# Local attention in a fused six-layer kernel: the loop over layers written out, and the weight split of a layer spread over two steps

## What is computed

```python
for i in range(DEPTH):
    x = attn_layer(shift_tokens(x), Wqkv[i], q_scale[i], k_scale[i], Wo[i]) + x
    x = ffn_layer(shift_tokens(x), ln_g[i], ln_b[i], W1[i], b1[i], W2[i], b2[i]) + x
...
def attn_layer(x, Wqkv, qs, ksc, Wo):
    qkv = x @ Wqkv                       # Wqkv is 128 x 3072
    ...                                  # l2norm of q and k, rotation, local attention
    return out @ Wo
```

## Time and profile before

| | us |
|---|---|
| median of 3 runs | 4807.92 (4804.89 to 4809.58) |
| the profiled execution | 4799.15, its span 4797.3 |
| PE, DVE, ACT, POOL busy in the span | 4226.0, 4007.1, 3749.9, 3518.3 |
| phase B, first to last step mark | 573.7 to 4045.5 |
| a plain step, n odd and n even | 35.33 and 36.02 |
| the two steps after a convert step | 36.02 and 35.33 |

### The profile page before, as it was taken

The page is one execution under the profiler, slowest core; times in us unless marked ns, Lnnn a source line. Parts: engine busy times, 40 slices in busy tenths (PEclk is TensorE's granted clock), DMA queues, the critical chain, the costliest instruction groups (busy, mean ns, idle before and its releaser), DMA issues. The chain is left out here.

```text
span 4797.3 us, 131407 instructions
## 1 busy us (share of the span) xinstructions
PE 4226.0 (88%) x45166; PEld 3150.4 (66%) x45166; DVE 4007.1 (84%) x7658; ACT 3749.9 (78%) x11543; POOL 3518.3 (73%) x2504
## 2 busy tenths in 40 slices
PE   6988699998999989998889989999899998688887
PEld 3555477776777777776777767777677776354553
DVE  4776798888888888888888888898898895688887
ACT  2555588888888888888888888888888887677774
POOL 0100699988899888998989989899899995344444
PEclk9999799999999999999999999999999999788888
DMA  1000111111111111111111111111121111000000
GB/s 27 6 5 2 49 48 44 44 38 52 53 40 43 48 48 47 44 44 45 46 53 43 40 45 52 47 44 44 45 53 38 44 44 28 3 4 3 3 3 5
DMA packets 118641, 169.38 MB, mean 35 GB/s; under 512 B 26563, under 2 KB 44422, under 8 KB 118022
## 3 DMA queue, kind: packets, MB, share of 16 engines
q1 hardware_dynamic: 109246, 160.92, 12.7%
q10 hardware_dynamic: 8776, 0.45, 0.1%
HBM read 20.79 MB, written 2.10 MB: 5 GB/s over the span
## 5 line engine op out<-in xcount | busy, mean ns | idle before, releaser
L1377 POOL TENSOR_TENSOR b_w<-b_w,b_vt 128x512 f32<-128x512 f32 x768 | 1188.4, 1558 | 331.8 <-DVE b_vt L1289 184.1
L1381 POOL TENSOR_TENSOR b_rn<-b_ssm,all_neg_half 128x16 f32<-128x16 f32 x384 | 1171.7, 3051 | 32.0
L1174 ACT ACTIVATE b_Pr<-ps,b_nm 128x96 f32<-128x96 f32 x3072 | 1002.8, 353 | 3.4 <-DVE b_nm L1346 2.8
L1174 ACT ACTIVATION_READ_ACCUMULATOR b_Pr<-ps,b_nm 128x1 f32 x3072 | 677.1, 220 | 0.0
L1216 ACT ACTIVATE b_PT<-ps 96x512 f32<-96x512 f32 x768 | 458.1, 597 | 264.1 <-PE ps L1026 257.1
L1060 PE MATMUL ps<-b_Whi,b_xlo 128*128 128x512 f32 x1152 | 579.2, 503 | 61.7 <-DVE b_Wlo L1306 25.8
L989 PE MATMUL ps<-all_ident,b_w 128*128 128x128 f32 x3072 | 460.6, 281 | 182.3 <-DVE b_xtok L282 118.7
L1340 DVE TENSOR_TENSOR b_Pr<-b_Pr,b_rinv 128x384 f32<-128x384 f32 x768 | 547.0, 712 | 26.3
L1026 PE MATMUL ps<-all_ident,b_Pr 128*96 128x128 f32 x3072 | 479.2, 279 | 68.8 <-ACT b_PT L1216 47.1
L1287 DVE TENSOR_TENSOR b_w<-ps,until_b_rotab 128x512 f32<-128x512 f32 x768 | 524.0, 682 | 8.9 <-ACT b_sq L1193 5.4
L1346 DVE TENSOR_REDUCE b_nm<-ps 128x8 f32<-128x768 f32 x384 | 367.5, 957 | 190.8 <-PE ps L1015 184.6
(11 more groups left out here) (259 smaller groups left out, 9375.4 us busy)
## 6 DMA issues: line engine op xcount, KB each, us to landing
b_V<-b_Vraw SPq DMA_DIRECT2D x384, 192.0 KB, 2.6
b_V<-b_Vraw SPq DMA_DIRECT2D x384, 128.0 KB, 2.4
b_V<-b_Vraw SPq DMA_DIRECT2D x192, 64.0 KB
b_Wraw<-in_L_ffn_Wqkv SPq DMA_DIRECT2D x36, 256.0 KB, 3.4
b_Wo<-in_L_ffn_Wo SPq DMA_DIRECT2D x6, 512.0 KB, 4.5
a_xtok<-in_L_attn_hidden_states SPq DMA_DIRECT2D x16, 128.0 KB, 2.1
out<-c_xout SPq DMA_DIRECT2D x16, 128.0 KB, 1.8
b_W<-in_L_ffn_W SPq DMA_DIRECT2D x6, 341.0 KB, 3.3
```

The lines of the kernel that those rows point to most:

```text
L1174: last = nc.scalar.activation(s.Pr[:, r % 2, j, i], ps[:, S_BANK[j], i * KEYS:(i + 1) * KEYS], ACT.Exp, bias=s.nm[:, r, j, i:i + 1], accum ...
L1377: nc.gpsimd.tensor_tensor(rows, rows, s.vt[:, i % 4], ALU.add).then_inc(s.pool_add, 1)
L1381: nc.gpsimd.tensor_tensor(s.rn[:, j], s.ssm[:, j], g.neg_half[:, 0:HB], ALU.pow).then_inc(s.pool_r, 1)
```

## The change

Two things are done, both in phase B.

The function that lays out the steps has no hardware loop any more: all 100 steps are written out, and every wait, address and table index is a constant. `prefetch` is called in the same four-steps-in places.

The conversion of the chunks is spread over two steps. k = 0 and 1 of the next layer are converted in the step of a layer's last item (n = 16 l + 14), in slots 11 and 14, after the pieces that still use those columns (ACT waits for them by `proj_done`). In the convert step k = 2, 3, 4, 5 stand in slots 1, 4, 7, 10. The last two places of `CHUNKS` change over. The first layer has no step before it and converts k = 0 and 1 in its slot 0. SP's code, its order of transfers and the loads' own conditions are as they were.

```diff
--- before.py
+++ after.py
@@ -716,8 +716,10 @@
 QK_SLOT = {0: (0, 0), 2: (0, 2), 6: (1, 0), 8: (1, 2), 16: (0, 1), 17: (0, 3), 22: (1, 1), 24: (1, 3)}
 V_SLOT = {15: (0, 4), 21: (1, 4), 29: (0, 5), 30: (1, 5)}
 ROTATE_LAG, ADD_LAG = 2, 2
-CHUNKS = (0, 2, 4, 1, 5, 3)
-CONVERT_SLOT = {0: (0, 1), 4: (2,), 8: (3,), 10: (4,), 12: (5,)}
+CHUNKS = (0, 2, 4, 1, 3, 5)
+FIRST_SLOT = {0: (0, 1)}
+AHEAD_SLOT = {11: (0,), 14: (1,)}
+CONVERT_SLOT = {1: (2,), 4: (3,), 7: (4,), 10: (5,)}
 
 LATE_SLOT = {0: (0, 3), 4: (0, 1), 6: (1, 3), 7: (1, 1)}
 WO_SLOT = (11, 12)
@@ -772,8 +774,9 @@
 
 
 
-    def __init__(self, n, odd, front, tail, ffn, closing, half=None, convert=False, edge=None):
+    def __init__(self, n, odd, front, tail, ffn, closing, half=None, convert=False, edge=None, last=False):
         self.n, self.odd, self.front, self.tail, self.ffn, self.closing, self.convert, self.edge = n, odd, front, tail, ffn, closing, convert, edge
+        self.last = last
         every = len(spare_uses(True, True, True, True, True))
         if half is None:
             self.attn, self.vacant = stages_of(n)[1], n == 2
@@ -785,6 +788,17 @@
             start = sum(len(spare_uses(*stages_of(i))) for i in range(-1, 2))
             self.halves, self.first = every * half, start + (every if odd else 0) - 2 * every
 
+    def converted(self, slot):
+
+        pieces = []
+        if self.last:
+            pieces += [(self.front[0] + 1, k) for k in AHEAD_SLOT.get(slot, ())]
+        if self.convert:
+            if self.n == -1:
+                pieces += [(self.front[0], k) for k in FIRST_SLOT.get(slot, ())]
+            pieces += [(self.front[0], k) for k in CONVERT_SLOT.get(slot, ())]
+        return pieces
+
     def spare(self, use):
 
         i = self.first + self.uses.index(use)
@@ -807,31 +821,15 @@
 
 
 def phase_b_steps(engine, body, between=None):
-    def whole(n):
+    for n in range(-1, ITEMS + 3):
         stages = stages_of(n)
         items = [divmod(n + d, NB) if there and n + d >= 0 else None for d, there in zip((1, 0, -1, -2, -3), stages)]
-        body(Step(n, n % 2, items[0], items[2], items[3], items[4], convert=n == -1))
-
-    def inner(l):
-        for pair in range(1, NB // 2 - 1):
-            n, half = NB * l + 2 * pair + 1, NB // 2 * l + pair
-            body(Step(n, 1, (l, 2 * pair + 2), (l, 2 * pair), (l, 2 * pair - 1), (l, 2 * pair - 2), half))
-            body(Step(n + 1, 0, (l, 2 * pair + 3), (l, 2 * pair + 1), (l, 2 * pair), (l, 2 * pair - 1), half + 1))
-
-    for n in range(-1, 3):
-        whole(n)
-    with engine.Fori(0, DEPTH - 1) as l:
-        if between is not None:
-            between(l)
-        inner(l)
-        n, half = NB * l + NB - 1, NB // 2 * l + NB // 2 - 1
-        body(Step(n, 1, (l + 1, 0), (l, NB - 2), (l, NB - 3), (l, NB - 4), half, convert=True, edge=0))
-        body(Step(n + 1, 0, (l + 1, 1), (l, NB - 1), (l, NB - 2), (l, NB - 3), half + 1, edge=1))
-        body(Step(n + 2, 1, (l + 1, 2), (l + 1, 0), (l, NB - 1), (l, NB - 2), half + 1, edge=2))
-        body(Step(n + 3, 0, (l + 1, 3), (l + 1, 1), (l + 1, 0), (l, NB - 1), half + 2, edge=3))
-    inner(DEPTH - 1)
-    for n in range(ITEMS - 1, ITEMS + 3):
-        whole(n)
+        layer, at = divmod(n, NB)
+        if between is not None and at == 3 and 0 <= layer < DEPTH - 1:
+            between(layer)
+        edge = at + 1 if 1 <= layer < DEPTH and at < 3 else None
+        body(Step(n, n % 2, items[0], items[2], items[3], items[4], convert=items[0] is not None and items[0][1] == 0, edge=edge,
+                  last=items[0] is not None and items[0][1] == NB - 1 and items[0][0] + 1 < DEPTH))
 
 
 def phase_b(nc, g, d, ps):
@@ -1176,13 +1174,14 @@
                     last.then_inc(s.exp_done, 1)
 
                 for slot in range(STEP_SLOTS):
-                    if step.convert:
-                        for k in CONVERT_SLOT.get(slot, ()):
-                            c = CHUNKS[k]
-                            act.wait_ge(s.wqkv_in[k % RAW], 16 * (WCHUNKS // RAW) * step.front[0] + 16 * (k // RAW) + 16)
-                            if k == 0:
-                                wait(act, s.proj_done, N_PIECES * f)
-                            nc.scalar.activation(s.Whi[:, c * 512:(c + 1) * 512], s.Wraw[:, k % RAW], ACT.Copy).then_inc(s.whi_done, 1)
+                    for layer, k in step.converted(slot):
+                        c = CHUNKS[k]
+                        act.wait_ge(s.wqkv_in[k % RAW], 16 * (WCHUNKS // RAW) * layer + 16 * (k // RAW) + 16)
+                        if step.last:
+                            act.wait_ge(s.proj_done, N_PIECES * f + max(PIECE.index(at) for at in PIECE if (QK_SLOT.get(at) or V_SLOT[at])[1] == c) + 1)
+                        else:
+                            wait(act, s.proj_done, N_PIECES * f)
+                        nc.scalar.activation(s.Whi[:, c * 512:(c + 1) * 512], s.Wraw[:, k % RAW], ACT.Copy).then_inc(s.whi_done, 1)
                     if step.front is not None and slot in PIECE:
                         tt, c = QK_SLOT[slot] if slot in QK_SLOT else V_SLOT[slot]
                         k = PIECE.index(slot)
@@ -1299,11 +1298,10 @@
                                             ALU.mult).then_inc(s.normed_dve, 1)
 
                 for slot in range(STEP_SLOTS):
-                    if step.convert:
-                        for k in CONVERT_SLOT.get(slot, ()):
-                            cols = slice(CHUNKS[k] * 512, (CHUNKS[k] + 1) * 512)
-                            dve.wait_ge(s.whi_done, WCHUNKS * lf + k + 1)
-                            nc.vector.tensor_tensor(s.Wlo[:, cols], s.Wraw[:, k % RAW], s.Whi[:, cols].bitcast(F32), ALU.subtract).then_inc(s.w_ready, 1)
+                    for layer, k in step.converted(slot):
+                        cols = slice(CHUNKS[k] * 512, (CHUNKS[k] + 1) * 512)
+                        dve.wait_ge(s.whi_done, WCHUNKS * layer + k + 1)
+                        nc.vector.tensor_tensor(s.Wlo[:, cols], s.Wraw[:, k % RAW], s.Whi[:, cols].bitcast(F32), ALU.subtract).then_inc(s.w_ready, 1)
                     if step.tail is not None and slot == RES_SLOT:
                         bank = SPARE[step.spare(("wo", 0))[0]]
                         full_spare(("wo", 0))
```

## The result

| | before | after |
|---|---|---|
| median | 4806.26 us (4796.60 to 4812.96, 20 runs) | 4814.1 us (4807.79 to 4820.12, 20 runs) |
| ratio, 95% interval | | 1.0016 (1.0010 to 1.0023) |
| profiled span | 4797.3 us | 4806.0 us |

A forecast was written before the change was run, and what follows sets the result against it. No engine alone bounds the kernel; PE, DVE and POOL hand each other a full load. -15.7 + 5 x (1.5 + 2.3) + 0.5 = +3.8 us on the 4807.92 us median gives 4812 us, range 4794 to 4828.

The forecast's parts named there:

- the boundaries: Last item's step plus convert step between layers, five times: 5 x (1.5 + 2.3) us longer.
- the straight-line steps: 80 looped steps written out with constants: 0.103 us more per step, +8.2 us.
- The turns: Four turns of the loop over layers vanish in straight-line code: -23.9 us.
- the rival of instruction supply: Twice the code, instruction supply stalls engines now and then: +10 to +20 us in all; chance 0.04.
- The last item's step: Two products moved ahead of DVE's residual add: +1.5 us a layer, bounds 1.0 and 1.9.
- The convert step: First step of a layer: PE's 2.31 us wait goes, a load wait comes; 2.3 us longer, bounds 0.6 and 3.5.
- The stall and its price: Convert step, slot 4: ACT waits 9 to 10 us for chunk 3's load, converting at +14.35; residual add at +30.2.
- the prediction's signs: Expected trace signs: convert step 50 us, ACT's third b_Whi idle 8 to 11 us, load 3.5 us behind first copy.
- The clock rival: PE at half clock after its convert-step idle time becomes the bound: 5 x 3 = 15 us more, 4827 us; chance 0.21.
- The free boundary: DVE catches up later or moved products fall into waits: boundary costs zero, sum -15.2, 4793 us; chance 0.13.
- The page's rule alone: Turns go and straight-line steps are as fast as looped ones: -23.9, 4784 us; chance 0.05.

The follow-up runs named there:

- Experiment 1: Against the changed kernel: all steps still written out, but the six conversions in their old slots and the old chunk order; 4780.62 us, 0.9959 of before.
- Experiment 4: Against the changed kernel: k = 2, 3, 4, 5 back in slots 4, 8, 10, 12; k = 0 and 1 stay ahead; 4777.75 us, 0.9949 of before.
- Experiment 6: Against the changed kernel: the last item's step has DVE's two products in slot 24 and both ACT conversions in slot 11; ratio 0.9990 to before.
- experiments 2: Against the changed kernel: loads of k = 3 and 4 issued early, in the last item's step between its two groups of copies; ratio 0.9947 to before.
- Experiment 3: Against the changed kernel: 84 unread transposes added on PE behind the values of slot 6 in five convert steps; 4821.08 us, 1.0042 of before.

## Why the prediction was right, and which of its terms were off

The forecast of a small loss made of a real gain and a larger cost held, and the time after, 4814.1, is 2 us from the 4812 named. Some of that nearness is luck: the median of before that it started from lay 1.7 us above the one over 20 runs, and two errors went against each other, the boundaries 9.1 us too cheap and the straight-line steps 4.5 too dear. In differences it is less close: +3.8 forecast, +7.7 in the medians and +8.7 in the profiled executions. Step by step:

**The turns** went as worked out: -23.0 for -23.9. The trace shows the price of a turn here, 5.3 to 6.6 us, and no row shows that the doubled straight-line code cost anything of that size elsewhere: the rival of instruction supply is out. The Trainium skill (Runtime: NRT & Kernel Launch, Instruction fetch mechanics) says that a taken branch breaks the sequential prefetch. The trace agrees in that the idle time stands at the turn; that fetching is what fills it is not shown.

**Straight-line steps** cost less than the term said. A pair of plain steps is 71.52 instead of 71.35, 0.08 us a step for 0.103. Of the 80 steps of that term 18 stand in the other rows of the table, 8 at the turns and 10 at the boundaries; for the 62 left it forecast 6.4 us, and 3.9 were measured, also because before's trace has one step of 36.55 (n = 43) that after's has not. What the 0.08 us consist of is not shown. Experiment 1 gives the term and the turns together as -20 us (forecast -15.7).

**The last item's step** is 38.26 where before has 36.01, so 2.25 us longer, for a forecast of 1.5 and above its upper bound of 1.9. The residual add comes 2.4 us later in the step than the earlier trace rows has it. The wait for ACT at slot 14 that the sum had is there, 0.40 us. What it lacked is that the second product takes 1.30 us and not 0.6, beside POOL's product. The rows had both durations; I had taken the short one.

**The convert step** is where the sum failed by size: +3.7 each for +2.3, just over the upper bound of 3.5. Its working can be followed row by row. The load reached ACT 6.2 us after the values of slot 6, not 7.24: the first load is issued 3.16 us behind the first copy instead of 3.48, and ACT has it 2.98 us after that instead of 3.72. Experiment 1, with before's slots, has 6.1 to 6.2 us in three convert steps and 7.1 and 7.2 in the two where the issue of one load took 1.5 and 1.7 us, so this belongs to the straight-line code and not to the slots. So ACT converted chunk 3 at +13.60 (13.4 to 14.0 in the five), where +14.35 was forecast, and DVE's product stood at +14.26. The add should then have come half a microsecond or more before the forecast +30.2; it came at +31.26. From the product on: 0.61 for it, 11.25 of the plain step, 0.61 and 1.31 for the two further products, 2.42 for the second wait, 0.87 saved where the plain step's b_Pr product (1.43 us beside POOL, 0.56 alone) now runs alone; that makes 14.26 + 0.61 + 11.25 + 1.92 + 2.42 - 0.87 = +29.6. The missing 1.6 is one instruction. The copy L1240 (L1241 before), before and after, over the whole trace (shortest, median, longest ns):

```profile
L1241 DVE TENSOR_SCALAR b_xhi<-all_xT x97: 291/291/294, 504.5 to 3989.4; 64x255 fp32r<-64x255 f32 x97
```

```profile
L1240 DVE TENSOR_SCALAR b_xhi<-all_xT x97: 290/291/1902, 505.7 to 3999.4; 64x255 fp32r<-64x255 f32 x97
```

Before it never took more than 0.294 us. After, it takes 1.90 in the convert steps, and POOL's normalisation lies exactly beside it:

```profile
1687.71 1.90 DVE L1240 TENSOR_SCALAR b_xhi<-all_xT 64x255 fp32r<-64x255 f32 x1
1684.46 2.93 POOL L1379 TENSOR_TENSOR b_rn<-b_ssm,all_neg_half 128x16 f32<-128x16 f32 x1
1687.47 1.99 POOL L1364 TENSOR_TENSOR b_w<-b_w,b_rn 128x1024 f32<-128x1024 f32 x1
```

I counted the collision of DVE and POOL that the stall removes (0.9) and not the one that it creates. The stall shifts POOL's chain of slot 4 against DVE's own order, and its normalisation now meets DVE's small copies. In a plain step that normalisation lies beside DVE's rotations, which read PSUM (ps) and keep their 0.68 us. Experiment 4, without the long stall, has no such long copy. Experiment 6 has one on the same instruction, and experiments 2 and 3 on b_xlo: 2.00 and 2.07 us for 0.42. The Trainium skill (SBUF — State Buffer, Who interferes with whom) says that DVE's second pair of ports is shared with GpSimd as an exclusive lock, that a DVE instruction with two SBUF inputs contends with a GpSimd one that reads SBUF, and that copies and tensor_scalar can enter modes that do. The durations agree with it; that it is this lock is argued from them, not shown by a run that only shifts POOL.

**The stall and its price.** ACT waits 9.1 to 9.6 us in all five steps (9 to 10 forecast), DVE a second time for 2.42 (1.7 to 2.4), and the load is issued 3.16 us behind the first copy (3.5). The conversion that waits is the second of the step, not the third as the prediction's signs have it. The convert step is 51.3, not 50. Experiments 2 and 4 settle that this stall is the cause: take it away at either end, by an earlier load or by later slots, and the convert steps together are 32 us shorter.

**The clock rival**, to which I had given 0.21, had its sign of the result and not its mechanism. Granted clock in the convert step is 0.87 (0.93 before), at half for 13.7 us in each; in two of the five 3.4 of these lie behind the add. In the step shown PE does the work in question at half clock for 5.4 us ahead of the add, more than the 3.5 that the rival asked for, and yet PE does not become the bound: just ahead of the add, at 1696.06, it waits 1.25 us for DVE again. Experiment 3 puts the price of this at 0.4 us a step, and the two falls behind the add cost 0.9 each: 3.8 us in all, where the rival had 15. That a fall behind the add lengthens the step is read from steps with and without one, in one kernel; no run sets the clock alone. **The free boundary** is refuted by the step lengths: nothing is caught up behind a boundary, and the plain steps are 35.47 and 36.05 throughout. **The page's rule alone** gave -23.9: its premise on the turns holds, and experiment 1, at -20, comes within 4 us of it; it says nothing of the chunks.

Still open is what brings the falls of the clock behind the add. In the convert steps of after and of experiments 2, 3 and 6, the stretch from the add on takes 20.0 us without one, 20.8 to 20.9 with 3.4 us at half clock around or behind the add and 21.9 to 22.3 with 6.8, but no run tells why one step has it and its neighbour has not.

## What to carry to other kernels

A conversion cannot be moved earlier than its load: before a consumer is put in an earlier slot, find the issue of its transfer in the queue and what stands ahead of it there, since the wait only changes its place and takes along all that the engine's order has behind it. Extra work belongs where its engine already waits for another; two products cost nothing ahead of the scores' maximum, and 2.2 us ahead of the residual add. After any stall, follow also the engine that shares something with the stalled one, because its long instruction will then meet others than before.

## What the runs showed of the hardware that I had not expected

- A DVE copy of 64x255 in SBUF takes 0.29 us alone and 1.90 beside a POOL product of 128x1024 that takes 1.99; DVE's 128x512 product of two SBUF tiles goes from 0.69 to 1.30 to 1.40 beside POOL's 128x512 one. DVE operations that read PSUM keep their time beside the same POOL instructions (0.68).
- Filling PE's idle time with 84 transposes kept the granted clock at full speed for over 22 us, and it then fell to half after the filled stretch, for 3.4 to 6.8 us, behind the add, where the step took 0.8 to 2.3 us longer than one at full speed.
- Half clock for 10 us and more in a stretch where DVE sets the pace costs 0.4 us; 3.4 us of it behind the add go with 0.9 us.
